# One attention stage of a two-layer kernel: row sums in two groups of matmuls instead of three, eight key tiles per chunk summed by DMA instead of seven, and value matmuls caught up at other steps

## The reference

```python
qkv = jnp.einsum('oc,bchw->bohw', w_qkv, x)
q, k, v = map(reshape, jnp.split(qkv, 3, axis=1))        # (b, 8, 32, 4096)
scores = jnp.einsum('bhdi,bhdj->bhij', q, k) / jnp.sqrt(d)
attn = jax.nn.softmax(scores, axis=-1)
out = jnp.einsum('bhij,bhdj->bhdi', attn, v)
x = jnp.einsum('oc,bchw->bohw', w_proj, out) + x
```

## Time and profile before

| | |
|---|---|
| three runs | 2570.38, 2570.99, 2572.07 us |
| the profiled execution | 2573.04 us |
| its span | 2571.3 us |
| mean granted TensorE clock | 0.991 of full speed |
| PE busy | 2501.2 us (97%) |
| ACT busy | 2283.3 us (89%) |
| DVE busy | 2174.5 us (85%) |
| POOL busy | 403.8 us (16%) |
| DMA queue of the adding DMAs | 44.8% of the 16 engines' span |

### The profile page before, as it was taken

The page is one execution under the profiler, slowest core; times in us unless marked ns, Lnnn a source line. Parts: engine busy times, 40 slices in busy tenths (PEclk is TensorE's granted clock), DMA queues, the critical chain, the costliest instruction groups (busy, mean ns, idle before and its releaser), DMA issues.

```text
span 2571.3 us, 58529 instructions
## 1 busy us (share of the span) xinstructions
PE 2501.2 (97%) x25050; PEld 719.3 (28%) x25066; DVE 2174.5 (85%) x1418; ACT 2283.3 (89%) x2574; POOL 403.8 (16%) x588
## 2 busy tenths in 40 slices
PE   7999999999999999999999999999899999999998
PEld 3222222242222222244442222222422222223443
DVE  6899999978999999796578999999789999997954
ACT  7999999989999999566589999999899999994663
POOL 0211121101122111110001212111021112120100
PEclk9999999999999999999999999999999999999999
DMA  2666566615566656301226566665166566661011
GB/s 104 124 124 129 119 126 124 130 35 122 127 125 124 130 118 128 61 1 68 85 54 124 122 127 123 125 130 119 45 123 129 117 129 124 128 124 32 1 58 42
DMA packets 85061, 262.36 MB, mean 102 GB/s; under 512 B 17616, under 2 KB 18704, under 8 KB 84528
## 3 DMA queue, kind: packets, MB, share of 16 engines
q0 software_dynamic: 64512, 234.91, 44.8%
q1 hardware_dynamic: 20288, 23.72, 2.8%
HBM read 14.75 MB, written 8.68 MB: 9 GB/s over the span
## 4 chain that ended last, share of the span: by engine, by line
PE 92%; ACT 4%; DVE 2%; issue 1%; DMA 1%; POOL 0%; ACTq 0%; SPq 0%; DVEq 0%; POOLq 0%
PE psOL L456 37%; PE psOL L445 29%; PE psOL L857 6%; PE scores L304 3%; PE scores L756 2%; ACT arena L527 2%; PE scores L315 2%; PE psOL L783 1%; PE psOL L418 1%; PE psOL L431 1%; PE psOL L424 1%; PE scores L445 1%; PE scores L844 1%; PE scores L845 1%; PE scores L834 1%
## 5 line engine op out<-in xcount | busy, mean ns | idle before, releaser
L567 DVE TENSOR_TENSOR arena<-arena 128x2048 f32<-128x2048 f32 x736 | 1686.7, 2292 | 116.7 <-PE psOL L418 35.2
L527 ACT ACTIVATE arena<-scores 128x1536 f32<-128x1536 f32 x1024 | 1588.8, 1552 | 0.0
L456 PE MATMUL psOL<-arena 128*32 128x512 f32 (+1 forms) x8960 | 1073.8, 567 | 1.4 <-ACT arena L527 1.4
L445 PE MATMUL psOL<-arena 32*128 32x512 f16 x3072 | 839.9, 379 | 22.3 <-ACT arena L526 17.7
L445 PE MATMUL scores<-arena 32*128 32x512 f16 x9216 | 846.4, 379 | 0.0
L526 ACT ACTIVATE arena<-psOL 128x512 f32<-128x512 f32 x1024 | 706.4, 690 | 30.0 <-PE scores L445 30.0
L597 POOL DMA_DIRECT2D arena<-arena x384 | 335.7, 995 | 1230.0 <-ACT arena L527 1023.2
L445 PEld LDWEIGHTS psOL<-arena 32*128 32x128 f16 x3072 | 206.9, 93 | 977.7 <-ACT arena L526 848.3
L456 PEld LDWEIGHTS psOL<-arena 128*32 128x32 f32 x8960 | 196.5, 108 | 474.7 <-issue 438.8
L445 PEld LDWEIGHTS scores<-arena 32*128 32x128 f16 x9216 | 220.1, 92 | 0.0
L857 PE MATMUL psOL<-arena 128*128 128x512 f16 x768 | 170.3, 379 | 0.0
(11 more groups left out here) (115 smaller groups left out, 1427.0 us busy)
## 6 DMA issues: line engine op xcount, KB each, us to landing
arena<-arena POOLq DMA_DIRECT2D x448, 512.0 KB, 5.5
X<-in_x SPq DMA_DIRECT2D x16, 512.0 KB, 4.6
out<-arena SPq DMA_DIRECT2D x32, 256.0 KB, 2.0
arena<-pool_inv SPq DMA_DIRECT2D x2, 2048.0 KB, 7.0
arena<-in_w_qkv SPq DMA_DIRECT2D x1, 768.0 KB, 4.6
Ls<-L SPq DMA_DIRECT2D x32, 8.0 KB
att_inv<-Ls SPq DMA_DIRECT2D x32, 8.0 KB
arena<-in_W_w SPq DMA_DIRECT2D x2, 256.0 KB, 2.8
```

The source lines that it names most:

```text
L445: last = nc.tensor.matmul(dst[h], K[rows, kp, j * 128:(j + 1) * 128], Q[rows, qp, cs], start=(n == 0), stop=(n == 2))
L456: last = nc.tensor.matmul(both[h * D:(h + 1) * D, lo:hi], V[:, j, h * D:(h + 1) * D], P[:, r + h, lo:hi], start=(j == 0), stop=(j == JT - 1))
L527: nc.scalar.activation(P[:, r + 1:r + G, :], bank[n % 2].rearrange("p (u n) -> p u n", n=CH), ACT.Exp, scale=SCORE).then_inc(s_exp, 1)
L567: nc.vector.tensor_tensor(acc[:], old, P[:, r:r + G, :], ALU.add).then_inc(s_add, 1)
```

## The change

Four things change, all in the attention stage.

1. `SUM_D` has eight tiles (2, 6, 9, 13, 16, 20, 23, 27) instead of seven, and no tile is left to PE. DVE still does 23 adds per chunk, since tile 31 is now one of its own.
2. `sums_of_tile` is gone. `sums_of_dma` comes first, at step 1 of the next chunk, and opens the accumulation; `sums_of_acc` follows at step 2 and closes it. Step 0 has no row sums. `s_sum` counts two per chunk.
3. The copy of `both` to `O` on DVE moves ahead of the chunk's last add (tile 31). DVE's first add of the next chunk waits for both groups of row sums, since the second group is the one that reads `acc`.
4. The values are caught up at single steps: 6, 10, 14, 18, 22 and 26. In the first chunk of a stage, which has no row sums ahead of it, they begin at step 1 and are caught up at steps 12 and 22. The matmuls on half tiles grow from 768 to 3008 instructions in the order's count (a tile has four such in each half): three tiles of every chunk were split, now twelve are, and ten in the first chunk of a stage.

```diff
-SUM_D = [3, 7, 11, 16, 20, 24, 29]
-SUM_PE = JT - 1
-SUM_V = [j for j in range(SUM_PE) if j not in SUM_D]
+SUM_D = [2, 6, 9, 13, 16, 20, 23, 27]
+SUM_V = [j for j in range(JT) if j not in SUM_D]
 ADDS = len(SUM_V) - 1
-PV_FROM = 3
-PV_MORE = [9, 10, 17, 18, 25, 26]
+PV_FROM = [1] + [3] * (NC - 1)
+PV_MORE = [[12, 22]] + [[6, 10, 14, 18, 22, 26]] * (NC - 1)
...
             def sums_of_acc(pe, c):
-                pe.wait_ge(s_o_free, c + 1)
                 pe.wait_ge(s_add, (c + 1) * ADDS)
                 for h in range(G):
-                    last = nc.tensor.matmul(both[h * D:(h + 1) * D, :], ones[:], acc[:, h, :], start=True, stop=False)
+                    last = nc.tensor.matmul(both[h * D:(h + 1) * D, :], ones[:], acc[:, h, :], start=False, stop=True)
                 last.then_inc(s_sum, 1)
...
             def sums_of_dma(pe, c):
+                pe.wait_ge(s_o_free, c + 1)
                 for k in range(2):
                     pe.wait_ge(s_dma[k], 16 * len(SUM_D) * (c + 1))
...
-                    if i == 0 and c:
+                    if i == 1 and c:
+                        sums_of_dma(pe, c - 1)
+                    if i == 2 and c:
                         sums_of_acc(pe, c - 1)
-                    if i == 1 and c:
-                        sums_of_tile(pe, c - 1)
-                    if i == 2 and c:
-                        sums_of_dma(pe, c - 1)
...
             def tensor_end(pe):
+                sums_of_dma(pe, NC - 1)
                 sums_of_acc(pe, NC - 1)
-                sums_of_tile(pe, NC - 1)
-                sums_of_dma(pe, NC - 1)
...
                 for c in range(NC):
-                    if c:
-                        output_out(dve, c - 1)
                     for n in range(ADDS):
                         j = SUM_V[n + 1]
+                        if j == JT - 1:
+                            output_out(dve, c)
                         dve.wait_ge(s_exp, 2 * (c * JT + j) + 2)
                         r = (c * JT + j) % RING * G
                         if n == 0:
                             if c:
-                                dve.wait_ge(s_sum, (c - 1) * 3 + 1)
+                                dve.wait_ge(s_sum, c * 2)
```

More of the change, by code:

```diff
@@ L41, with halves_by @@
 LAG = 2
-SUM_D = [3, 7, 11, 16, 20, 24, 29]
-SUM_PE = JT - 1
-SUM_V = [j for j in range(SUM_PE) if j not in SUM_D]
+SUM_D = [2, 6, 9, 13, 16, 20, 23, 27]
+SUM_V = [j for j in range(JT) if j not in SUM_D]
 ADDS = len(SUM_V) - 1
-PV_FROM = 3
-PV_MORE = [9, 10, 17, 18, 25, 26]
+PV_FROM = [1] + [3] * (NC - 1)
+PV_MORE = [[12, 22]] + [[6, 10, 14, 18, 22, 26]] * (NC - 1)
 def adds_through(j):
     return max(1, sum(1 for t in SUM_V if t <= j) - 1)
-def halves_by(i):
-    return sum(3 if k in PV_MORE else 2 for k in range(PV_FROM, i + 1))
+def halves_by(c, i):
+    return sum(3 if k in PV_MORE[c] else 2 for k in range(PV_FROM[c], i + 1))
 TERMS = [(0, 0), (0, 1), (1, 0)]
@@ L68 @@
     SIDES_AT[(_s - FIRST) * (JT - 1) // (len(SIDES) - FIRST)].append(_s)
-assert SUM_V[:2] == [0, 1] and halves_by(JT - 1) == 2 * JT and JT % RING == 0
+assert SUM_V[:2] == [0, 1] and all(halves_by(c, JT - 1) == 2 * JT for c in range(NC)) and JT % RING == 0
 Part = namedtuple("Part", "tensor tensor_end scalar vector vector_end gpsimd sync sems signals")
@@ L430, in sums_of_dma @@
                 for h in range(G):
-                    last = nc.tensor.matmul(both[h * D:(h + 1) * D, :], ones[:], accD[:, h, :], start=False, stop=True)
+                    last = nc.tensor.matmul(both[h * D:(h + 1) * D, :], ones[:], accD[:, h, :], start=True, stop=False)
                 last.then_inc(s_sum, 1)
@@ L481, in tensor @@
                         nc.tensor.transpose(both[0:1, 0:128], bound[:, 2:3], ident[:, :]).then_inc(s_tr, 1)
-                    if i == 0 and c:
+                    if i == 1 and c:
+                        sums_of_dma(pe, c - 1)
+                    if i == 2 and c:
                         sums_of_acc(pe, c - 1)
-                    if i == 1 and c:
-                        sums_of_tile(pe, c - 1)
-                    if i == 2 and c:
-                        sums_of_dma(pe, c - 1)
-                    at, end = halves_by(i - 1), halves_by(i)
+                    at, end = halves_by(c, i - 1), halves_by(c, i)
                     while at < end:
@@ L509, in slot_free @@
                         act.wait_ge(s_dma[k], 16 * (c * len(SUM_D) + SUM_D.index(j) + 1))
-                elif j == SUM_PE:
-                    act.wait_ge(s_sum, c * 3 + 2)
                 else:
@@ L534, in sums_out @@
             def sums_out(dve, c):
-                dve.wait_ge(s_sum, (c + 1) * 3)
+                dve.wait_ge(s_sum, (c + 1) * 2)
                 if c:
@@ L572, in vector @@
                             nc.vector.reciprocal(Ls[:, g, c - 1:c, :], Ls[:, g, c - 1:c, :]).then_inc(s_inv, 1)
-                output_out(dve, NC - 1)
             def vector_end(dve):
@@ L590, in gpsimd @@
                                 if c:
-                                    pool.wait_ge(s_sum, c * 3)
+                                    pool.wait_ge(s_sum, c * 2 - 1)
                                 elif ahead:
-                                    pool.wait_ge(ahead.signals["sum"], NC * 3)
+                                    pool.wait_ge(ahead.signals["sum"], NC * 2 - 1)
                                 nc.gpsimd.dma_start(dst, src).then_inc(s_dma[k], 16)
@@ L716, in gpsimd @@
                 if b is not None:
-                    pool.wait_ge(behind.signals["sum"], NC * 3)
+                    pool.wait_ge(behind.signals["sum"], NC * 2)
                 nc.gpsimd.memset(TB[CM:128, :].bitcast(F32), 0.0).then_inc(s_pad, 1)
```

## The result

The changed kernel takes 2617.2 us (median of 4 runs, 2616.47 to 2617.28) against 2570.77 us (median of 4 runs of the kernel before, 2570.38 to 2572.07): a ratio of 1.0177, 95% interval 1.0165 to 1.0189, 46 us slower. Its mechanism is there; one of its terms, the falls of the clock at the borders, was more than twice too large.

A forecast was written before the change was run, and what follows sets the result against it. ACT was taken to bound plain steps by 0.07 us, PE the catch-up steps. Terms 47.6 - 4.4 - 5.4 + 21 = +59 us on the profiled 2573.0 gave 2632, against the median 2630; 80% range 2602 to 2662.

The forecast's parts named there:

- What bounds, and the border: At 28 chunk borders the copy to L stands behind DVE's add, PE's values wait, ACT loses 2.03 us each.
- Rival C: At the borders the copy to L doesn't hold PE; kernel faster, -24 us, 2547 us; chance 6%.
- The catch-up: Single catch-up steps in border chunks lose 0.88 us against 1.21 for pairs, 0.33 gained; border chunk 1.70 more, 47.6 in all.
- The split tiles: 280 more value tiles split in halves, eight more instructions each: taken as costing nothing, bound 49 us.
- Rival D: Split value tiles cost what their added weight loads take, up to 49 us on the forecast, 2679 us; chance 7%.
- The third group: Removing the third group of row sums at a chunk's start gains nothing; it stood in a step without values.
- the eighth DMA tile: One more tile summed by DMA per chunk costs nothing; its DMAs fit within the chunk; bound 84 us.
- The start of a stage: Values from step 1 in first chunks: 5.4 us of clock falls gained, plus 4.4 us from first chunks' catch-up.
- The falls at the borders: PE's 2.4 us pause halves the clock at 14 of 28 borders, about 1.5 us each: 21 us, bounds 0 and 42.
- Rival A: The border stall comes without falls of the clock: +38 us, 2609 us; chance 27%.
- Rival B: The border stall with a clock fall at nearly every border, some longer: +80 to +95 us, 2650 to 2665; chance 10%.
- The ends of the stages: At four stage ends, one group less (1.07 us) but a 2.29 us add behind the copy to `O`: 0, bounds -4 and +9.

The follow-up runs named there:

- the copy moved: Changed kernel with DVE's copy to L put ahead of the chunk's first add instead of behind it: 2558.6 us, ratio 0.9951 to the kernel before.
- the stall alone: Kernel before with one number changed, DVE's first add of a chunk waiting for all three groups of row sums: 2637.85 us, ratio 1.0263.
- The first chunk alone: Kernel before with the new values' numbers only in each stage's first chunk (from step 1, catch-up at 12 and 22): 2563.84 us, ratio 0.9972.
- the new values' schedule alone: Kernel before with only the values' schedule numbers changed to the new ones, three row-sum groups and seven DMA tiles kept: 2550.11 us; repeated, 2551.23 us.
- the kernel with values from step 2: Changed kernel with copy to L ahead of the first add, row sums at steps 0 and 1, values from step 2, four single catch-ups: 2550.78 us.
- the last add moved: Kernel with copy to L first, row sums at steps 0 and 1, values from step 2, plus each stage's last add put into `vector_end`: 2547.97 us.
- the kernel with the old values' schedule: Changed kernel with the values from step 3 and catch-up pairs as before, two row-sum groups and eight DMA tiles kept: 2636.97 us, ratio 1.0251.

## Why the prediction was right

**What bounds, and the border.** Right, to a tenth of a microsecond: 4.90 and 5.90 us against 5.04 and 6.00, 1.94 lost on ACT against 2.03. Of the 0.14 less, 0.08 came from the copy, which starts that much before the add ahead of it is listed as ended, and 0.05 from the sums of `acc`, which start 0.75 into their step instead of 0.80. Rival C, that the copy doesn't hold PE, needed a wait under 0.3; it was 2.25. Two experiments show it as a cause, not only as a place: the copy moved, and the stall alone.

**The catch-up.** Right: 2.04 us for the first single after the stall (0.21 lost), 1.96 or 1.97 for the later ones (0.13 lost), 59.35 us a chunk without a stall against 59.4. A border chunk cost 1.56 more against 1.70; 28 of them 43.7 against 47.6.

**The split tiles.** Right to take nothing: 864 split tiles more cost 0 to 0.19% of the time, at most 0.006 us each against the bound of 0.18. "TensorE: Matmul & The Clock Gate" of the Trainium skill, section "Back-to-back issue gap", has the spacing set by both the loads and the matmuls. The measurement differs: in this stream 1.8 times the loads (15872 against 8960) cost under 0.2%, and it decides. Rival D is refuted.

**The third group, and the eighth DMA tile.** Right that neither costs anything by itself (61.81 against 61.80 us a chunk with the stall, 59.35 against 59.35 without), but the text priced the eighth tile by its DMAs only. Its worth is on DVE: without it DVE bounds the chunk (59.65 us and more). The DMAs stayed hidden, at 5.6 us from issue to landing:

```profile
DMA to landing us min/median/max: 4.5/5.6/6.8
```

**The start of a stage.** 9.8 us forecast with the first chunks' catch-up. The first chunk alone gave 7, since one fall still cost 1.2 and the way to the second image gave less than forecast; in the changed kernel no fall stands at the start of a stage.

**The falls at the borders.** This is the mis-sized term. The price of a fall was right, 1.58 against 1.5. The count was taken as half, from two of four pauses in layer 1; it was 5 of 28, so 8 us instead of 21. Rival A had named the reason for fewer, that whether a border has a fall may be the same at border after border. The runs bear that out in part: in each stage of the changed kernel the first stretch is 63.01 us, the second stretch of the second stage is 62.94, and all others but the last ones are 61.43. Where the chunk is 61.80 or 61.81 us there are eight and nine long ones, partly at other borders. What decides at a given border stays open. Rival B, a fall at nearly every border, didn't come. Four pauses, in another layer with other work around them, were too few to take a share from.

**The ends of the stages.** Zero forecast, within -4 and +9; about zero in sum, from parts of both signs, so that the agreement is luck. With the first chunk's 1.1 and the fall of the kernel before (2.1, in one of the two) taken out, each of the two hand-overs inside an image is 3.0 us longer: 104.68 and 104.69 against the 101.71 twice of the new values' schedule alone. Two things make this up. DVE's first work for the second projection stands behind the last add, and the row sums there run at half clock: eight matmuls of one group take 1.95 us instead of 1.04. PE in the first hand-over of the changed kernel, where the copy to O started at 538.31 (the granted clock from 543.8 to 547.2 is 0.51):

```profile
542.92 1.17 PE L424 MATMUL psOL<-arena,ones 128*32 128x512 f32 x8
543.84 1.95 PE L416 MATMUL psOL<-arena,ones 128*32 128x512 f32 x8
...
547.72 0.22 PE L314 MATMUL scores<-wq_hi,arena 128*128 128x128 f16 x1
```

and in the kernel with values from step 2, which has the same order on DVE in this place and no fall there; its copy to O started at 522.61:

```profile
527.22 1.06 PE L424 MATMUL psOL<-arena,ones 128*32 128x512 f32 x8
528.11 1.04 PE L416 MATMUL psOL<-arena,ones 128*32 128x512 f32 x8
...
530.38 0.22 PE L314 MATMUL scores<-wq_hi,arena 128*128 128x128 f16 x1
```

From the copy to the first matmul of line 314 that is 9.41 and 7.77 us; with the new values' schedule alone it is 6.43, and with the last add moved 6.38. So the add costs some 1.3 to 1.4 us in each of these hand-overs, and the fall 1.6. Moving the add gave back its share; that the whole stretch became 3 us shorter is also owed to falls that this profile doesn't have.

The hand-over to the second image, with first chunk and fall taken out, is 4.1 us shorter, and the profiles point to the clock here too, though no experiment was made on it: the changed kernel and the one with the copy moved have no fall right behind the last copy of the second stage and take 327.02 us both, while all profiles with one (3.4 to 13.7 us long) take 330.2 to 334.8. Tail and start give 1.4 and 1.1 more. The falls outside the borders were in no term of the forecast but that for the starts of the stages.

**Outside the span.** Not forecast: 2.6 us more in the profiled execution. It is there in all runs of the changed kernel and of those with the copy moved (4.1 to 5.1 us), and not in the kernel with the old values' schedule or in the one with the new schedule alone (1.6 to 2.9). Neither the number of instructions nor the order of row sums alone makes it. It stays open.

The sum, term by term: 43.7 for the chunks and 0.5 for the last stretches, 8 for the falls at the borders, about -10 for starts, first chunks and the ends together, 2.6 outside the span, 44 between the two profiled executions. With 5 falls in place of 14 the forecast's 59 would have been 45; the border, 47.6 for 43.7, is the largest of what is left, and the 2.6 outside the span, not forecast, hide most of it.

## What to carry to other kernels

When a wait is moved to a later event, list what stands behind the waiting instruction on its engine and who waits for that: here one count of a semaphore put a 2.3 us add between a finished result and the copy that another engine needed, 28 times. Where two instructions wait for the same event, the one that others wait for goes first. A term that removes work on the busiest engine is worth nothing until something uses the free place; here that took moving the row sums and the values one step ahead (a chunk of 58.98 instead of 59.35 us). And where a profile shows falls of the clock, look for them before a stretch that became longer or shorter is put down to an edit: a fall of 3.4 us cost 1.6 us in the hand-over, the add 1.3 to 1.4.

## What the runs showed of the hardware

A pause of TensorE of 2.25 us between dense matmuls was followed by a half clock of 3.4 us at some borders and not at others of the same kernel, at a cost of 1.58 us; three of four stages ran with one such fall in seven equal pauses, one with two. Splitting nearly all value matmuls from 512 to 256 columns, with 1.8 times the weight loads, changed the busy time of the matmuls by 0.3%. VectorE's copy behind an add started 0.08 us before the add is listed as ended.
